# Four-layer cross-attention stack on one Trainium2 core: the projections and feed-forward products issued as column tiles of 32 stationary columns

## The reference, cut to what matters

```python
Q, K, V = x @ Wq + bq, kv @ Wk + bk, kv @ Wv + bv        # split into heads
attn = softmax(Q @ K^T / sqrt(d_head) + masks)
x = layernorm(x + (attn @ V) @ Wo + bo) * g + b
```

## Time and profile before

| | |
|---|---|
| median of three runs | 2382.64 us |
| the profiled execution | 2381.61 us |
| its span, first to last instruction | 2379.7 us |
| TensorE matmul busy | 2337.2 us (98%), 30353 instructions |
| TensorE weight loads busy | 1970.0 us (83%), 30353 instructions |
| DVE busy | 1499.7 us (63%) |
| ACT busy | 1377.1 us (58%) |
| POOL busy | 948.4 us (40%) |
| granted TensorE clock, mean | 0.999 of full speed |

### The profile page before, as it was taken

One profiled execution on the slowest core, in us unless ns is written; L12 is line 12 of the kernel. 1 busy time (PEld: TensorE's weight loads), 2 busy tenths in 40 slices (PEclk: granted clock), 3 DMA queues, 4 the chain that ended last, 5 costly groups with the idle time before them and its releaser, 6 DMA issues.

```text
span 2379.7 us, 74174 instructions
## 1 busy us (share of the span) xinstructions
PE 2337.2 (98%) x30353; PEld 1970.0 (83%) x30353; DVE 1499.7 (63%) x3091; ACT 1377.1 (58%) x3238; POOL 948.4 (40%) x1764
## 2 busy tenths in 40 slices
PE   8999999999999999999999999999999999999998
PEld 7788888888778888888877888888887788888887
DVE  7886644446888664444688866444478877544446
ACT  5566665545556666554555666654465565655555
POOL 3565422224447432223345743222334574322233
PEclk9999999999999999999999999999999999999999
DMA  5300000000100000000010000000001000000000
GB/s 184 110 2 3 2 2 1 1 1 17 38 5 2 3 2 2 1 1 2 21 37 2 2 3 3 2 1 1 1 25 34 2 2 3 2 1 2 1 1 20
DMA packets 23794, 32.53 MB, mean 14 GB/s; under 512 B 2304, under 2 KB 22176, under 8 KB 23328
## 3 DMA queue, kind: packets, MB, share of 16 engines
q1 hardware_dynamic: 23456, 27.78, 3.6%
HBM read 23.57 MB, written 4.19 MB: 12 GB/s over the span
## 4 chain that ended last, share of the span: by engine, by line
PE 91%; issue 4%; POOL 3%; DVE 2%; DMA 0%; POOLq 0%; ACT 0%; SPq 0%; DVEq 0%
PE M L581 53%; PE SC L777 15%; PE M L587 10%; PE M L811 6%; PE SC L793 3%; PE M L828 3%; PE SC L625 2%; POOL Kx L1338 1%; POOL Y L1374 1%; DVE nmax L1217 0%; POOL seen_diag L1365 0%; POOL q L1325 0%; DVE Kx L1196 0%; DVE stats L1284 0%; POOL rstd L1386 0%
## 5 line engine op out<-in xcount | busy, mean ns | idle before, releaser
L581 PE MATMUL M<-XT,W 128*128 128x128 f32 x4096 | 520.5, 277 | 0.8 <-DMA W<-w_k 0.7
L581 PEld LDWEIGHTS M<-XT,W 128*128 128x128 f32 x4096 | 486.6, 192 | 12.1 <-issue 3.1
L1217 DVE TENSOR_REDUCE nmax<-SC 128x8 f32<-128x1024 f32 x320 | 390.7, 1221 | 125.5 <-PE SC L777 124.3
L1338 POOL TENSOR_SCALAR Kx<-K,own,k_ones 128x128 f32<-128x128 f32 x640 | 294.1, 472 | 260.5 <-PE SC L777 220.1
L983 ACT ACTIVATE Pr<-SC 128x1024 f32<-128x1024 f32 x256 | 262.4, 1025 | 221.7 <-PE SC L777 221.7
L777 PE MATMUL SC<-Kx,Qx 32*128 32x128 f32 x5120 | 364.4, 280 | 11.3 <-issue 7.2
L777 PE MATMUL SC<-Qx,Kx 32*128 32x128 f32 x5120 | 371.2, 283 | 0.0
L777 PEld LDWEIGHTS SC<-Kx,Qx 32*128 32x128 f32 x5120 | 315.9, 186 | 65.5 <-issue 48.7
L777 PEld LDWEIGHTS SC<-Qx,Kx 32*128 32x128 f32 x5120 | 310.2, 186 | 2.4 <-issue 1.4
L953 ACT ACTIVATE Qx<-M,q_bias,q_scale 128x128 f32<-128x128 f32 x640 | 240.5, 458 | 108.7 <-PE M L581 108.6
L1386 POOL TENSOR_SCALAR rstd<-mv 128x1 f32<-128x1 f32 x256 | 103.5, 404 | 483.1 <-DVE mv L1289 482.9
(11 more groups left out here) (145 smaller groups left out, 4137.6 us busy)
## 6 DMA issues: line engine op xcount, KB each, us to landing
X<-x SPq DMA_DIRECT2D x32, 128.0 KB, 2.1
c_in<-ctx_in SPq DMA_DIRECT2D x32, 128.0 KB, 2.2
out<-X SPq DMA_DIRECT2D x32, 128.0 KB, 1.7
RV<-row_vec SPq DMA_DIRECT2D x1, 2304.0 KB, 8.7
W<-w_k SPq DMA_DIRECT2D x5, 256.0 KB, 3.7
W<-w_q SPq DMA_DIRECT2D x5, 256.0 KB, 4.0
W<-w_v SPq DMA_DIRECT2D x5, 256.0 KB, 4.0
W<-w_f SPq DMA_DIRECT2D x1, 1024.0 KB, 5.3
```

The source lines that it names most:

```text
L581: last = pe.matmul(dst, a, b, start=(k == 0), stop=(k == len(lhsTs) - 1))
L1217: dve.tensor_reduce(nm, SC[h][:, :].rearrange("p (g c t) -> p g c t", c=KC, t=P), AX_X, ALU.max, negate=True).then_inc(maxima, 1)
L1338: last = pool.tensor_scalar(kx[:, half_of, c * P:(c + 1) * P], k[:, c * P:(c + 1) * P], own[:, half_of:half_of + 1], k_ones[:, half_of, c: ...
```

## The change

A helper `column_tiles` takes the place of `product` in `by_weight` (items `K`, `Q`, `F1`), in `by_tokens` (items `V`, `E3`, `F2`, `BV`) and in item `L`. It issues each product of 128 stationary columns as four products of 32 stationary columns, each into its own 32 partitions of the same PSUM tile, with the same streamed operand. `product` stays for the small `BC` items at the start. Order of items, waits, buffers, data types and everything on the other engines are as before.

```diff
@@ -44,6 +44,7 @@
 TILES = 4
+TILE_COLS = 32
@@ -587,21 +588,28 @@
+            def column_tiles(dst, lhsTs, rhss):
+                for k, (a, b) in enumerate(zip(lhsTs, rhss)):
+                    for t in range(0, P, TILE_COLS):
+                        last = pe.matmul(dst[t:t + TILE_COLS, :], a[:, t:t + TILE_COLS], b, start=(k == 0),
+                                         stop=(k == len(lhsTs) - 1), skip_group_check=True)
+                return last
+
             def by_weight(it, name, src, tiles, first=0):
@@
-                    last = product(tile_of(it)[:, j * P:(j + 1) * P],
-                                   [weight(name, k, m, m + P) for k in range(KC)],
-                                   [src[:, k * P:(k + 1) * P] for k in range(KC)])
+                    last = column_tiles(tile_of(it)[:, j * P:(j + 1) * P],
+                                        [weight(name, k, m, m + P) for k in range(KC)],
+                                        [src[:, k * P:(k + 1) * P] for k in range(KC)])
@@
-                product(tile_of(it)[:, 0:n], parts,
-                        [weight(name, k, at, at + n) for k in range(len(parts))]).then_inc(tile_full, 1)
+                column_tiles(tile_of(it)[:, 0:n], parts,
+                             [weight(name, k, at, at + n) for k in range(len(parts))]).then_inc(tile_full, 1)
@@ -745,8 +753,8 @@
-                    product(tile_of(it)[:, 0:P], [q[:, c, :] for c in range(KC)],
-                            split(k, KC)).then_inc(tile_full, 1)
+                    column_tiles(tile_of(it)[:, 0:P], [q[:, c, :] for c in range(KC)],
+                                 split(k, KC)).then_inc(tile_full, 1)
```

## The result

The changed kernel takes 2447.99 us (2447.72 to 2448.39, four runs) where the kernel before takes 2382.3 us (2381.87 to 2383.28, four runs). The ratio is 1.0276, with a 95% interval of 1.0261 to 1.0292: 65.7 us slower. The profiled execution took 2447.91 us, its span is 2446.1 us.

The account below looks back on a forecast made before the run. TensorE's list of items was taken as the bound. Onto the profiled 2381.6 us came +75.0 (shape changes +90.4, pitch -15.4), waits -6 and 1.0 to the median: 2452 us, range 2433 to 2490.

Parts of the forecast that it names:

- The bound: Whole kernel: it is as long as TensorE's list of items, TensorE being busy for 98% of the span.
- Pitch: Line 581: 6144 instructions with 128 streamed columns become rounds 0.0025 us shorter each, -15.4 us; 256 columns taken as 0.
- Changes of shape: TensorE's list: 2068 switches between whole array and column tiles or other shapes instead of 1353, +90.4 us.
- Waits: TensorE: waits for POOL's `q` at `L` partly vanish, those at the scores stay, -6 us; bounds 0 and 35 us.
- POOL `q` under 4 us: TensorE's list of waits after the change: those for POOL's `q` should total under 4 us, from 8.5 before.
- the step from the profiled execution to the median: Kernel before: the profiled execution took 1.0 us under the median, so 1.0 us was added to the sum.
- The check: Same accounting on the list before: 2355 us, with 35 us of waits 2390 against a span of 2379.7, 0.4% off.
- the range of the sum: Whole kernel: 2435 to 2465 us, from 0 to 20 us of waits taken up and +-6 us for 256-column rounds; chance 0.76.
- A: TensorE's feed: instructions don't come fast enough above 27 ns a pair; 2500 us at 40 ns, 2960 at 53; chance 0.11.
- B: TensorE's list: switching shape costs nothing more, so the shorter rounds win, 2367 us with nothing paid; chance 0.04.
- C: Line 581's rounds: four tiles can't stream the same operand together, a round costs four times, 3.7 ms more; chance 0.02.
- D: TensorE: existing waits and overlapping drains take up much of the loss, all 35 us vanish, 2420 us; chance 0.07.

Follow-up runs that it names:

- E3: Not a run label in itself: the output projection item. The run with only this item in column tiles of 32, against the kernel before: 2400.32 us.
- the kernels by parts: Changed kernel with only some items in column tiles: V, E3, F2, BV 2440.69 us; K, Q, F1 2433.80; E3 alone 2400.32; attention 1 alone 2392.81.
- the two halves: Changed kernel with column tiles of 32 only in V, E3, F2, BV: 2440.69 us; only in K, Q, F1: 2433.80 us.
- the tiles of 64: Changed kernel with column tiles of 64 columns in place of 32 for every item, two products instead of four: 2456.41 us.
- the kernel with swapped loops: Changed kernel with the two loops of column_tiles swapped, so one tile gets all its parts before the next: 2981.49 us.

## Why the prediction was right

The forecast was 2452 us, range 2433 to 2490; 2447.99 was measured. By its steps:

- **The bound.** TensorE's list sets the end: right, 94% of the chain.
- **Pitch** (the distance from one instruction or round to the next), **-15.4 us.** A round of 0.109 for 128 columns is confirmed. The unknown rounds of 256 columns take 0.216, the value taken; those of 512 take 0.429, as whole-array instructions do. Their bounds of +-6 us were not needed.
- **Changes of shape, +90.4 us.** Confirmed in number (leaving the whole array 515 to 679 times, leaving column tiles 161 to 711) and in size, at each place where I looked: 0.093, 0.024, 0.114, and 0.33 instead of 0.27 for the transpose behind. It was the term with the weight, and the prices read around `PV` alone held for items of other kinds. List and stalls together leave a remainder of -2.5 us. It is -1.3 to -2.5 in the kernels by parts as well and hardly grows with the number of split instructions (896 to 8596); where it comes from stays open.
- **Waits, -6 us.** The net was -6.1, but the step got there by luck, by errors that cancel. It said that the wait at `L` vanishes, some 6 us, and that those at the scores stay. In truth `L` gave back 7.3 and the scores took 3.5 of it again, with 2.3 from the start and small ones. The sign that was named for this step, POOL `q` under 4 us, was missed: 5.0 us are listed. The mechanism (excursions take up a wait of 0.2 us) was right. Its base was mis-sized, for the list of waits shows 8.5 us where the distances show 17.9 at `L`, and nothing was thought of what gets late behind `L`.
- **The error that is left**, 2452 - 2448 = 4 us: 2.5 from the remainder, 1.0 from the step from the profiled execution to the median (0.1 us in the kernel after), the rest rounding.
- **The check** of the list before (2355, with 35 us of waits 2390 against 2379.7) is weaker than it looks. From the first start to the last there are 2369.9 us, 48.1 of them stalls, so the list took some 2322, 33 less than 2355. The two kernels must share nearly all of that error, since their difference is off by 2.5 us only; where it lies stays open. And the range of the sum, 2435 to 2465, is 3 us short below: 2457.6 - 20 - 6 = 2432.

The rivals. *A*, feed: 27.5 ns a pair over 128 pairs without a gap. Over 1024 pairs the densest stretch has 37.9 ns a pair, before 54.5. At the rates of this kernel the feed costs nothing; what it would cost above them stays open. *B*, free changes: refuted by the sum, and the two halves that don't add up. *C*, one operand for four tiles: rounds of 0.109, not 0.43. *D*, waits that take up much: the stalls fell by 6 us of 48. In its place stands a weaker form of it that the tiles of 64 show: an added 91 us took up 14.5.

## What to carry to other kernels

Column tiles of a stationary operand that fills the array gain 2% of the streaming at best (0.1092 against 0.1117 us with 128 streamed columns, nothing with 256 or 512), and each change between them and whole-array work costs 0.1 us out and 0.06 to 0.1 back; so count the changes in the list before the instructions, and give an item the shape of its neighbours (here worth 15 us, where one shape for all lost 66). Read what a step on TensorE costs from start to start, for neither the busy time of a group nor idle time shows it. If an item is moved to save a change, look at the list of the engine that empties it: moved on TensorE's list alone it cost 35 us.

## What the hardware showed that was not expected

- **Matmuls start out of the order of the list.** A matmul for a free column tile starts ahead of waiting ones for a busy tile, across the border of two items (`V` in `F2`, above). Four pairs in a row for one tile don't hold the line, eight do (2.3 times the time) and sixteen (3.2 times). The Trainium skill (TensorE: Matmul & The Clock Gate, Part 2, Step-by-step) says that "The MATMULs themselves stay in program order"; the rows of the kernel with swapped loops show otherwise for tiles of different columns, and go before it.
- **The price of entering goes with the length of the first weight load:** 0.024 us for 32 columns, 0.050 for 64, 0.102 to 0.104 for 128 (0.101 to 0.103 in the cost tables above), but 0.056 for a transpose, which has 128 columns too. The mean weight loads of the kernel before (109, 136, 140 and 190 ns in the lines below) are each 0.084 to 0.088 us longer than these prices:

```profile
L811 PEld LDWEIGHTS M<-Pr,V 128*32 128x32 f32 x5120 | 130.0, 109 | 24.6 <-issue 9.2 <-DVE ne L1185 3.7
L828 PEld LDWEIGHTS M<-Pr,V 128*64 128x64 f32 x1024 | 54.6, 136 | 7.7
L587 PEld LDWEIGHTS M<-ident,OT 128*128 128x128 f32 x640 | 70.3, 140 | 15.0
L581 PEld LDWEIGHTS M<-W,OT 128*128 128x128 f32 x512 | 94.8, 190 | 12.0
```

- **Leaving costs the same from every float32 shape:** where nothing waits, the first matmul of the next shape starts 0.200 to 0.205 us after the last one with 128 streamed columns, be it from the whole array, from tiles of 32 or 64 columns or from the row tiles of the scores (0.31 us after one with 256).
- **A small matmul and its weight load cost 27.5 ns together** when four tiles take turns, 128 in a row. The Trainium skill (TensorE: Matmul & The Clock Gate, Part 2, Back-to-back issue gap) gives some 81 ns for one matmul of 128 streamed columns in a stream of loads and matmuls; `F1` shows a third of it where each has a quarter of the array. (A float32 pair on the whole array takes 112 ns in this kernel.)
- **The instruction stream grows** from 3.96 to 7.26 MB, and no wait for it shows (`F1`, the densest item, has no gap):

```profile
q8 instruction: 443, 7.26, 1.3%
```
